# Register values of the tensor engine in rows of eight words, and an even share of aggregation behind every group, in a graph network kernel

## The chip, the core and the metric

The kernel runs on one core of a Trainium2 chip. The metric is the device time of one execution in microseconds, as the median of several runs. TensorE (PE) multiplies matrices, VectorE (DVE) does element-wise work and reductions, ScalarE (ACT) copies, scales and evaluates functions, GpSimd (POOL) sets constants up here, and SyncE (SP) starts most transfers. Each engine works through its own instructions in their order; semaphores tie the engines together. An instruction whose address is known only at run time takes it from a register, and a TENSOR_LOAD fills registers with values from on-chip memory.

## The reference: what is computed

3125 nodes with 128 features each, 53125 edges (src, dst, type), sorted by dst. Two blocks follow each other:

```
agg  = segment_sum((x[src] + rel_emb[type]) @ W_msg.T + b_msg, dst) / max(deg, 1)
x    = layernorm(x + x @ W_self.T + b_self + agg)
h    = swish(segment_mean(x[src], dst) @ W1_l.T + b1 + x @ W1_r.T)
out  = layernorm(x + segment_mean(h[src], dst) @ W2_l.T + b2 + h @ W2_r.T)
```

So one graph is used three times: three times a sum over each node's incoming edges, and behind each a small dense step.

## The kernel before

**Edges become a matrix of counts.** `A` (the profile calls it counts) holds in f16 how many edges lead from each source node to each destination node, 25 blocks of 128 sources by 3125 destinations. It is made from 416 tiles of 128 edges. Four tiles are a group, so there are 104 groups. For each group DVE writes one-hot rows (`one_hots`, L1165 to L1181) into one of two, from group 12 on one of three, buffers; it may refill a buffer when PE has signalled `released` for the group that used it. PE turns the rows into counts with some 20 small matmuls (`count`, L878 to L932: blocks L894, types L901, shared columns L910 and L930) in a window of PSUM, and ACT copies that window into `A` in two halves (L837), with `copied` signalled to PE.

**Run-time places.** Where a tile's 12 columns stand within the group's window of 38 is data. DVE computes it (L1128) into `place_i`, three int32 per group, for the tiles 1 to 3 (tile 0 always stands at 0). PE loads the values for two groups (`LOADED = 2`), six words or 24 bytes, ahead of every even group (L1040), 52 loads in all. ACT loads the first column of eight groups' windows at once (L828), eight words or 32 bytes. The built program puts `place_i` at an address that is a multiple of 32 bytes, so PE's loads start alternately on a multiple of 16 and on 8 bytes beside one.

**Work behind the groups.** As edges are sorted by destination, the first columns of `A` are complete long before the last group. `spread()` plans which blocks of the first aggregation (`aggregate`, L945: table block times counts, two matmuls of 256 columns per block, since the table holds each value as a high and a low part) stand behind which group. Five chunks of 512 nodes are cut into eleven parts of 256 columns, 25 blocks each. A part may start only from the group `READY[part] + 1` on. The number of blocks behind a group is `4 - group % 2`: four behind an even group, three behind an odd one, none behind the four groups of `OWN`, fewer where dense steps (`dense`, L1011 and L1021, `count_degrees`, L977) are planned behind the same group. When all 25 blocks of a part are placed, the next part waits for its `READY`. What has not been placed by group 103 is done right after the loop. The functions `lead`, `scale`, `root`, `normalise` of ACT and `degrees`, `add_up`, `measure`, `combine`, `invert`, `low` of DVE follow the groups given by that same plan.

**The rest.** After group 103 the other chunks and the two later layers run, 50 matmuls of 512 columns per chunk, with the dense steps between them. Four weights are loaded by SP into the memory of the one-hot rows when the last group has been copied (L705). Biases are loaded at the start (L699). A check that the plan holds for these edges runs on DVE (`check_edges`) while PE aggregates layer 1.

Of the kernel before, what the change touches and what calls it, by code (L numbers as in the profile page):

```python
# [15 lines left out]
P = 128  # L16
N = 3125
D = 128
# [63 lines left out]
def spread():  # L82
# [5 lines left out]
    for group in range(GROUPS):  # L88
        room = 0 if group in OWN else 4 - group % 2
# [92 lines left out]
def gnn_program(nc, x, src_t, dst_t, type_t, first_dst, rel_emb, w_msg, w_self, w1_l, w1_r,  # L182
                w2_l, w2_r, b_self, b_msg, b1, b2, x1_dram, h_dram, out):
    with ExitStack() as ctx:
# [5 lines left out]

        A = sb("counts", [P, BLOCKS, WIDTH], F16)
# [12 lines left out]
        base_i = sb("base", [P, GROUPS], I32)  # L204

        place_i = sb("place", [P, GROUPS, GROUP - 1], I32)
        weights_first = sb("weights_first", [P, 2, D])
        bias_rows = sb("bias_rows", [P, 3, D])
# [10 lines left out]
        std = sb("std", [P, SUB])  # L219
        offset = sb("offset", [P, SUB])  # L220
        eps_col = sb("eps_col", [P, 1])
        peaks = sb("peaks", [P, PEAKS])
        limits = sb("limits", [P, PEAKS])
        over = sb("over", [P, PEAKS])
        any_over = sb("any_over", [P, 1])
        ones_col = sb("ones_col", [P, 1])
        flag = sb("flag", [P, 1], I32)
# [23 lines left out]
        assert 4 * D + 2 * CHUNK + TILES + GROUPS <= (SLOTS - 1) * HOT_C * GROUP // 2  # L251

        ident = new_first[:, 0:P]
        bias_msg = scaled_flat[:, 0:D]

        def by_tile(buffer):
            return buffer.rearrange("p (g t) -> p g t", t=GROUP)
# [422 lines left out]
        def _(sp):  # L680
# [16 lines left out]
            for to, b in ((bias_rows[:, 0, :], b_self), (bias_msg, b_msg),  # L697
                          (bias_rows[:, 1, :], b1), (bias_rows[:, 2, :], b2)):
                sp.dma_start(to, b.rearrange("o d -> (o d)").partition_broadcast(P)  # L699
                             ).then_inc(weights_in, 16)  # L700
# [18 lines left out]
        def _(pool):  # L719
# [11 lines left out]
            nc.gpsimd.memset(peaks[:], 0.0)  # L731
            for at, most in ((slice(0, 1), (TILE_W - 1) / 2), (slice(1, 2), -1.0),
                             (slice(2, 3), 0.0), (slice(3, 5), float(TILE_W)),
                             (slice(5, 7), 0.0), (slice(7, 8), MOST_VALUE),
                             (slice(8, 9), MOST_EDGES / 2 - 1),
                             (slice(9, 10), (TYPE_W - 1) / 2),
                             (slice(10, PEAKS), MOST_VALUE / SCALE)):
                last = nc.gpsimd.memset(limits[:, at], most)
            last.then_inc(constants, 1)
# [139 lines left out]
        def _(pe):  # L879
# [116 lines left out]
            def dense(q, tiles):  # L996
                layer, size = layer_of(q), min(P, nodes_of(q))
                if 0 in tiles:
                    pe.wait_ge(sum_ready, q + 1)
                    pe.wait_ge(own_ready, max(q + 1, POSTED))  # L1000
                    if before(q) >= 0:
                        pe.wait_ge(messages_scaled, before(q) + 1)
                        if q >= POSTED:
                            pe.wait_ge(y_ready, before(q) + 1)
                    if q == CHUNKS:
                        pe.wait_ge(late_weights_in, 64)
                    if q >= POSTED:
                        pe.wait_ge(preset_done, q + 1 - POSTED)
# [29 lines left out]
            for group in range(GROUPS):  # L1038
# [5 lines left out]
                mine = group % LOADED * (GROUP - 1)  # L1044
                count(group, places[mine:mine + GROUP - 1])
# [44 lines left out]
        def _(dve):  # L1090
# [18 lines left out]
            def of_groups(count=GROUP):  # L1109
# [18 lines left out]
            nc.vector.tensor_tensor(place_i[:], by_tile(start_i)[:, :, 1:GROUP],  # L1128
                                    of_groups(GROUP - 1), ALU.subtract
# [65 lines left out]
            def constant(step):  # L1195
# [5 lines left out]
                elif step == 1:  # L1201
                    dve.wait_ge(weights_in, 16 * 6)
                    nc.vector.tensor_tensor(weights_first[:, 1, :], weights_first[:, 1, :],
                                            ident, ALU.add).then_inc(weights_ready, 1)
                elif step == 2:
                    nc.vector.tensor_tensor(bias_rows[:, 0, :], bias_rows[:, 0, :], bias_msg,
                                            ALU.add).then_inc(weights_ready, 1)
# [17 lines left out]
            def preset(q):  # L1225

                layer, size = layer_of(q), min(P, nodes_of(q))
                bias = bias_rows[0:size, layer, :]
# [17 lines left out]
            def store_own(q):  # L1246
# [6 lines left out]
                    bias_rows[:, 0, :].unsqueeze(1).to_broadcast([P, SUB, D]), ALU.add  # L1253
# [76 lines left out]
            def check_edges():  # L1330
# [14 lines left out]
                                               -(TILE_W - 1) / 2, place_i[:, 0:early],  # L1345
# [4 lines left out]
                                               place_i[:, early:GROUPS, 0:GROUP - 2],  # L1350
# [4 lines left out]
                                               place_i[0:REST, early:GROUPS, GROUP - 2],  # L1355
# [6 lines left out]
                for t in range(GROUP):  # L1362
# [23 lines left out]
                nc.vector.tensor_copy(within[:, :, 0], place_i[:, :, 0]).then_inc(check_step, 1)  # L1386
                nc.vector.tensor_tensor(within[:, :, 1:GROUP - 1], place_i[:, :, 1:GROUP - 1],
                                        place_i[:, :, 0:GROUP - 2], ALU.subtract
                                        ).then_inc(check_step, 1)
                nc.vector.tensor_tensor(steps[:, 0:early], steps[:, 0:early],  # L1390
                                        place_i[:, 0:early, GROUP - 2], ALU.subtract
# [9 lines left out]
                for h in range(EARLY_PARTS):  # L1401
# [13 lines left out]
                                        place_i[:, GROUPS - 1, GROUP - 2:GROUP - 1], ALU.subtract  # L1415
# [36 lines left out]
            for q in range(EARLY - 1, ALL_CHUNKS):  # L1452
                if EARLY <= q < CHUNKS:
                    degrees(q)
                if q == CHUNKS:
                    dve.wait_ge(agg_done, CHUNKS)
                    check_edges()
# [7 lines left out]
                if q == 2 * CHUNKS:  # L1465
                    dve.wait_ge(check_step, CHECKS + 1 + CHUNKS)
                    nc.vector.tensor_tensor(over[:], peaks[:], limits[:], ALU.is_gt
                                            ).then_inc(over_step, 1)
                    dve.wait_ge(over_step, 1)
                    nc.vector.tensor_reduce(any_over[:], over[:], AX.X, ALU.max  # L1470
# [61 lines left out]
```

## Time and profile before

| | us |
|---|---|
| median of 3 runs | 376.63 (376.56 to 378.17) |
| the profiled execution, its own time | 376.94 |
| its span, first to last instruction | 375.2 |
| PE busy | 340.1 (91%) |
| DVE busy | 239.5 (64%) |
| ACT busy | 175.2 (47%) |
| granted TensorE clock, mean | 0.992 of full speed |

The profiled execution is 1.74 us longer than its span and 0.31 us longer than the median. The shares over the span hide two very different stages: groups are counted from about 12 us to 189 us, where three engines are busy at once, and from there PE works nearly alone.

### The profile page before, as it was taken

What the parts mean: (1) busy time and instruction counts of PE and PEld (TensorE: products, weight loads), DVE (VectorE), ACT (ScalarE), POOL (GpSimd) and SP (SyncE); (2) the same over time, 40 slices, a digit from 0 to 9 for tenths busy, and PEclk for the clock granted to TensorE, in tenths of its full rate; (3) what the DMA queues carried; (4) which work ended last, traced back from release to release, by engine and by line L of the source; (5) the groups of instructions that cost most, each with busy time, mean ns of one, the idle gap of its engine ahead of it and who ended that gap; (6) DMA issues with size and microseconds to landing.
All of it is one profiled execution on the core that took longest, in us unless ns stands there. A gap on an engine that the chain in (4) does not pass through costs nothing.

```text
span 375.2 us, 9264 instructions
## 1 busy us (share of the span) xinstructions
PE 340.1 (91%) x3385; PEld 249.6 (67%) x3385; DVE 239.5 (64%) x666; ACT 175.2 (47%) x385; POOL 5.1 (1%) x26
## 2 busy tenths in 40 slices
PE   0579999998999999999899999999999999999980
PEld 0578898887888888888886445554565454555460
DVE  6999988988898998998635763303317013431445
ACT  1577666668767768668623204311334130221130
POOL 5000000000000000000000000000000000000000
PEclk9999999999999999999999999999999999999996
DMA  4700000000000000000010000000000000000102
GB/s 130 177 3 3 2 2 3 4 2 0 4 2 2 3 2 2 3 3 3 1 31 0 3 0 2 0 2 0 0 2 2 0 1 30 28 3 28 29 2 64
DMA packets 8523, 5.38 MB, mean 14 GB/s; under 512 B 370, under 2 KB 8476, under 8 KB 8476
## 3 DMA queue, kind: packets, MB, share of 16 engines
q1 hardware_dynamic: 8188, 4.32, 4.2%
q8 instruction: 31, 0.51, 0.6%
q10 hardware_dynamic: 288, 0.43, 0.5%
q14 instruction: 16, 0.13, 0.1%
HBM read 3.14 MB, written 1.60 MB: 13 GB/s over the span
## 4 chain that ended last, share of the span: by engine, by line
PE 80%; DVE 13%; issue 4%; ACT 1%; DMA 1%; DVEq 0%; ACTq 0%
PE ps L945 50%; PE ps L894 17%; PE ps L1011 5%; DVE hot L1181 3%; PE ps L1021 3%; PE ps L964 2%; DVE hot L1170 2%; DMA counts<-dst_t 1%; DVE table L1181 1%; PE ps L901 1%; PE ps L991 1%; PE ps L910 1%; DVE table L1191 1%; DVE stats L1276 1%; ACT scaled L793 1%
## 5 line engine op out<-in xcount | busy, mean ns | idle before, releaser
L945 PE MATMUL ps<-counts,table 128*128 128x256 f16 (+2 forms) x1350 | 215.7, 309 | 0.8 <-ACT sum_first L770 0.8
L945 PEld LDWEIGHTS ps<-counts,table 128*128 128x128 f16 x1350 | 114.3, 97 | 75.0 <-issue 1.1
L837 ACT CAST counts<-ps 128x494 f32 x208 | 107.6, 573 | 55.0 <-PE ps L894 54.6
L894 PE MATMUL ps<-hot 128*128 128x156 f16 (+1 forms) x584 | 70.4, 244 | 21.0 <-DVE hot L1181 15.2
L894 PEld LDWEIGHTS ps<-hot 128*128 128x128 f16 x584 | 53.4, 103 | 27.7 <-DVE hot L1181 16.5
L1181 DVE TENSOR_TENSOR hot<-iota,edges 128x1200 f16<-128x1200 f16 x73 | 56.6, 776 | 0.0
L1170 DVE TENSOR_TENSOR hot<-iota,edge_rows 128x768 f16<-128x768 f16 x73 | 40.3, 552 | 6.9 <-PE ps L930 6.6
L901 PE MATMUL ps<-hot 128*128 128x19 f16 x292 | 43.4, 181 | 0.0
L1269 DVE TENSOR_TENSOR new_first<-ps,scaled 128x512 f32<-128x512 f32 (+1 forms) x9 | 5.4, 599 | 54.0 <-ACT scaled L793 54.0
L1269 DVE TENSOR_TENSOR hot<-ps,scaled 128x512 f32<-128x512 f32 (+1 forms) x8 | 5.1, 638 | 41.9 <-ACT scaled L793 41.9
L894 PE MATMUL ps<-table 128*128 128x156 f16 (+1 forms) x248 | 28.8, 237 | 1.4 <-DVE hot L1181 0.5
L901 PEld LDWEIGHTS ps<-hot 128*128 128x128 f16 x292 | 29.2, 100 | 0.5
L770 ACT ACTIVATE sum_first<-ps 128x512 f32<-128x512 f32 (+1 forms) x13 | 7.0, 539 | 45.3 <-PE ps L945 45.3
L770 ACT ACTIVATE hot<-ps 128x512 f32<-128x512 f32 (+1 forms) x8 | 4.4, 548 | 48.1 <-PE ps L945 48.1
L793 ACT ACTIVATE scaled<-ps,rdeg 128x128 f32<-128x128 f32 (+1 forms) x75 | 21.6, 372 | 11.1 <-PE ps L1011 8.6
L894 PEld LDWEIGHTS ps<-table 128*128 128x128 f16 x248 | 21.8, 99 | 4.9 <-DVE hot L1181 2.2
L1181 DVE TENSOR_TENSOR table<-iota,edges 128x1200 f16<-128x1200 f16 x31 | 24.0, 775 | 0.0
L910 PE MATMUL ps<-next_hot,hot 128*128 128x13 f16 (+1 forms) x144 | 21.7, 185 | 0.0
L1170 DVE TENSOR_TENSOR table<-iota,edge_rows 128x768 f16<-128x768 f16 x31 | 17.1, 552 | 2.4 <-PE ps L930 2.1
L901 PE MATMUL ps<-table 128*128 128x19 f16 x124 | 17.8, 176 | 0.0
L910 PEld LDWEIGHTS ps<-next_hot,hot 128*128 128x128 f16 x144 | 14.4, 100 | 0.5
L1181 DVE TENSOR_TENSOR hot<-iota_type,edges 128x76 f16<-128x76 f16 x73 | 13.9, 190 | 0.0
(136 smaller groups left out, 320.1 us busy)
## 6 DMA issues: line engine op xcount, KB each, us to landing
table<-x SPq DMA_DIRECT2D x2, 768.0 KB, 5.2
out<-new_first SPq DMA_DIRECT2D x3, 256.0 KB
out<-hot SPq DMA_DIRECT2D x3, 256.0 KB, 2.3
counts<-first_dst ACTq DMA_DIRECT2D x1, 208.0 KB, 3.7
counts<-dst_t SPq DMA_DIRECT2D x1, 208.0 KB, 4.7
counts<-type_t ACTq DMA_DIRECT2D x1, 208.0 KB, 5.1
counts<-src_t SPq DMA_DIRECT2D x1, 208.0 KB, 5.2
bias_rows<-b SPq DMA_DIRECT2D x2, 64.0 KB, 4.4
```

What stands on the lines that cost most here:

```text
L770: nc.scalar.activation(sum_T(q)[:, 0:nodes], ps[:, sums_bank(q), 0:nodes], ACT.Copy, scale=1.0 / SCALE).then_inc(sum_ready, 1)
L793: last = nc.scalar.activation(scaled[0:part, t], ps[0:part, messages_bank(q), t * D:(t + 1) * D], ACT.Copy, scale=rdeg[0:part, tile:tile + 1])
L837: nc.scalar.copy(A[:, HALVES[half], bass.ds(bases[group % 8], GROUP_W)], window(group, half)).then_inc(copied[half], 1)
L894: return nc.tensor.matmul(window(group, half)[:, :, at[t]], row(tiles[t], LOW_AT, P), blocks_of(tiles[t], half), start=group == half == t ...
L901: return nc.tensor.matmul(relations(group)[:, column], row(tiles[t], TYPE_AT, P), row(tiles[t], WIN_AT, TYPE_W), start=group == t == 0, st ...
L910: nc.tensor.matmul(window(then, half)[:, :, 0:1], row(tiles[-1], LOW_AT, P), next_hot[:, group // NEXT % 2, HALVES[half], group % NEXT].un ...
L945: last = nc.tensor.matmul(ps[:, sums_bank(q), first:first + width], table[:, b, part, :], A[:, b, at:at + width], start=b == part == 0, st ...
L1011: sent = nc.tensor.matmul(ps[0:size, messages_bank(q), t * D:(t + 1) * D], sum_T(q)[:, at], weight(layer, 0), start=True, stop=True)
L1021: last = nc.tensor.matmul(to, own_T[:, at], weight(layer, 1), start=False, stop=False, skip_group_check=True)
L1170: nc.vector.tensor_tensor(rows[:, :, TYPE_AT + REL_ROW:M_AT, :].rearrange("p h (k c) t -> p h k c t", c=PIECE), iota[:, 0:PIECE, :].unsque ...
L1181: last = nc.vector.tensor_tensor(rows[:, :, at:at + width, :], numbers, edge[:, kind, group * GROUP:(group + 1) * GROUP].rearrange("p (h t ...
L1269: nc.vector.tensor_tensor(rows(new(q), q), from_own, rows(scaled, q), ALU.add).then_inc(y_ready, 1)
```

## The change

- `place_i` gets four int32 per group instead of three: the value of tile 0 is kept too (it is not used as an address). A row of two groups is eight words, 32 bytes, and PE's load takes all eight. `place_i` and `base_i` are moved in front of the other buffers; the built program puts `place_i` on a multiple of 32 bytes again, so every load starts on a multiple of 32 bytes.
- `spread()` has room for four blocks behind every group. 20 instead of 16 blocks of the eleventh part are placed inside the loop.
- To make room for it in memory, `b2` is no longer loaded at the start but after the four late weights, into the same memory as they; the wait of PE for these transfers and one of DVE take it in. `limits`, which POOL set at the start with nine memsets, lies in the memory of `next_block` and is set by DVE behind the seventh aggregation. Small buffers are put together. The check takes the extra word in: it multiplies the value of tile 0 by 128 and adds it to the next.

```diff
-        room = 0 if group in OWN else 4 - group % 2
+        room = 0 if group in OWN else 4
...
+        base_i = sb("base", [P, GROUPS], I32)
+
+        place_i = sb("place", [P, GROUPS, GROUP], I32)
         A = sb("counts", [P, BLOCKS, WIDTH], F16)
...
-        base_i = sb("base", [P, GROUPS], I32)
-
-        place_i = sb("place", [P, GROUPS, GROUP - 1], I32)
...
-        bias_rows = sb("bias_rows", [P, 3, D])
+        bias_first = sb("bias_rows", [P, 2, D])
...
+        bias_last = later[:, 4 * D + 2 * CHUNK + TILES + GROUPS:][:, 0:D]
...
+        limits = next_block[:].bitcast(F32)[:, 0:PEAKS]
...
             for k, w in enumerate((w1_l, w1_r, w2_l, w2_r)):
                 sp.dma_start(weights_later[:, k, :], w).then_inc(late_weights_in, 16)
+            sp.dma_start(bias_last, b2.rearrange("o d -> (o d)").partition_broadcast(P)
+                         ).then_inc(late_weights_in, 16)
...
-            nc.gpsimd.memset(peaks[:], 0.0)
-            for at, most in ((slice(0, 1), (TILE_W - 1) / 2), (slice(1, 2), -1.0),
...
-                last = nc.gpsimd.memset(limits[:, at], most)
-            last.then_inc(constants, 1)
+            nc.gpsimd.memset(peaks[:], 0.0).then_inc(constants, 1)
...
                     if q == CHUNKS:
-                        pe.wait_ge(late_weights_in, 64)
+                        pe.wait_ge(late_weights_in, 80)
...
-                mine = group % LOADED * (GROUP - 1)
-                count(group, places[mine:mine + GROUP - 1])
+                mine = group % LOADED * GROUP
+                count(group, places[mine + 1:mine + GROUP])
...
-            nc.vector.tensor_tensor(place_i[:], by_tile(start_i)[:, :, 1:GROUP],
-                                    of_groups(GROUP - 1), ALU.subtract
+            nc.vector.tensor_tensor(place_i[:], by_tile(start_i), of_groups(), ALU.subtract
                                     ).then_inc(place_ready, 1)
...
-                    dve.wait_ge(weights_in, 16 * 6)
+                    dve.wait_ge(weights_in, 16 * 5)
...
+                if q == 2 * CHUNKS:
+                    dve.wait_ge(late_weights_in, 80)
...
                 if q == CHUNKS:
                     dve.wait_ge(agg_done, CHUNKS)
+                    for at, most in ((slice(0, 1), (TILE_W - 1) / 2), (slice(1, 2), -1.0),
...
+                        nc.vector.memset(limits[:, at], most)
```

Two places on PE. The first is the end of group 15 and the start of group 16, before the change; table and hot are the buffers of one-hot rows, and x6 stands for six instructions alike.

```order
360 L894 ISA
361 L894 MATMUL ps<-table 128x12x12
362 L910 MATMUL ps<-next_hot,table 128x12 [waits copied1]
363 L930 MATMUL ps<-next_node,table 128x1
364 L945 MATMUL ps<-counts,table 128x256 x6
365 L1040 TENSOR_LOAD place
366 L894 MATMUL ps<-hot 128x13x12 [waits v_hot]
```

The same place after it:

```order
360 L890 ISA
361 L890 MATMUL ps<-table 128x12x12
362 L906 MATMUL ps<-next_hot,table 128x12 [waits copied1]
363 L926 MATMUL ps<-next_node,table 128x1
364 L941 MATMUL ps<-counts,table 128x256 x8
365 L1036 TENSOR_LOAD place
366 L890 MATMUL ps<-hot 128x13x12 [waits v_hot]
```

The load stands where it stood, between the aggregation of the odd group and the counting of the even one; two more matmuls of 256 columns stand ahead of it. The second place on PE is the end of the loop, before the change:

```order
2376 L894 ISA
2377 L894 MATMUL ps<-hot 128x12x12
2378 L945 MATMUL ps<-counts,table 128x256 x24
2379 L1032 MATMUL ps<-iota 128x512 [waits constants,copied1,copied0]
2380 L945 MATMUL ps<-counts,table 128x256 x50
```

And after it:

```order
2369 L890 ISA
2370 L890 MATMUL ps<-hot 128x12x12
2371 L941 MATMUL ps<-counts,table 128x256 x18
2372 L1028 MATMUL ps<-iota 128x512 [waits constants,copied1,copied0]
2373 L941 MATMUL ps<-counts,table 128x256 x50
```

Of the 24 matmuls six stood behind group 103 and 18 were what the loop had left; now eight stand behind group 103 and ten are left. So eight matmuls have moved into the loop. No instruction of PE is added or taken away.

## Rows read from the trace of the kernel before

**Rows 1.** Stretch, length, busy PE, PEld, DVE, ACT, POOL, clock, DMA share, GB/s.

```profile
34.00:186.00 152.00, 144.56 (x1970) 129.85 (x1968) 138.13 (x363) 108.96 (x229) 0.00 (x0) 1.00 0.01 2
...
206.00:375.20 169.20, 158.10 (x986) 87.43 (x984) 63.02 (x195) 41.77 (x105) 0.00 (x0) 0.98 0.04 11
```

**Rows 2.** Waits from 34 to 186 us: us in total, times, longest.

```profile
PEld ps L894 <- issue: 8.5, 17, 1.0
DVE hot L1170 <- PE ps L930: 6.3, 19, 0.7
PE ps L894 <- issue: 3.5, 5, 0.8
DVE next_hot L1165 <- PE ps L930: 2.9, 10, 0.5
PEld ps L894 <- DVE hot L1181: 2.6, 6, 0.7
DVE table L1170 <- PE ps L930: 2.1, 7, 0.5
PEld ps L894 <- DVE table L1181: 1.0, 1, 1.0
```

**Rows 3.** The chain of work, behind groups 19 to 22, 33 and 34: start, us, what.

```profile
48.09 0.68 PE ps L945 x6
49.51 0.90 PE ps L945 x8
51.16 0.68 PE ps L945 x6
52.97 0.90 PE ps L945 x8
...
70.90 0.68 PE ps L945 x6
71.58 0.65 issue
73.27 0.90 PE ps L945 x8
```

**Rows 4.** PE's loads: all, then one by one; ns min/median/max, first and last start.

```profile
L1040 PEldq TENSOR_LOAD <-place x52: 813/1240/1487, 8.3 to 184.6; - x52
...
L1040 PEldq TENSOR_LOAD <-place x1: 1474/1474/1474, 70.7 to 70.7; - x1
...
L1040 PEldq TENSOR_LOAD <-place x1: 814/814/814, 161.4 to 161.4; - x1
```

**Rows 5.** ACT's loads of eight words from 20 us on.

```profile
L828 ACTq TENSOR_LOAD <-base x12: 544/546/549, 28.3 to 175.6; - x12
```

**Rows 6.** Timeline: group 46's last one-hot row, and PE's first matmul of it.

```profile
89.30 0.19 DVE L1181 TENSOR_TENSOR hot<-iota_type,edges 128x76 f16<-128x76 f16 x1
...
92.47 0.23 PE L894 MATMUL ps<-hot 128*128 128x156 f16 x1 [0.73 <-DVE table L1181]
```

**Rows 7.** DVE's groups by line: busy, mean ns.

```profile
L1123 DVE TENSOR_TENSOR counts<-counts,base 128x416 int32<-128x416 int32 x1 | 0.6, 586 | 0.0
L1128 DVE TENSOR_TENSOR place<-counts,base 128x312 int32<-128x312 int32 x1 | 0.5, 473 | 0.0
```

**Rows 8.** The end of the loop, in order of time.

```profile
187.75 1.16 ACT L793 ACTIVATE scaled<-ps,rdeg 128x128 f32<-128x128 f32 x4
188.54 2.79 PE L945 MATMUL ps<-counts,table 128*128 128x256 f16 x24
188.76 1.07 ACT L837 CAST counts<-ps 128x494 f32 x2
```

**Rows 9.** A late weight's transfer: KB each, us to landing.

```profile
hot<-w_r SPq DMA_DIRECT2D x2, 64.0 KB, 2.0
```

**Rows 10.** Timeline of DVE in a chunk's first dense step.

```profile
101.89 0.69 DVE L1269 TENSOR_TENSOR new_first<-table,scaled 128x512 f32<-128x512 f32 x1
...
103.77 0.86 DVE L1276 BATCH_NORM_STATS2 stats<-new_first 128x6 f32<-128x128 f32 x4
```

More of the change, by code:

```diff
@@ L218, in gnn_program @@
         moments = sb("moments", [P, SUB, 2])
-        std = sb("std", [P, SUB])
-        offset = sb("offset", [P, SUB])
-        eps_col = sb("eps_col", [P, 1])
+        small = sb("small", [P, 16])
+        std, offset = small[:, 0:SUB], small[:, SUB:2 * SUB]
+        eps_col, any_over, ones_col = (small[:, k:k + 1] for k in range(8, 11))
+        flag = small[:, 11:12].bitcast(I32)
         peaks = sb("peaks", [P, PEAKS])
[L223 to L227, printed above, removed]
         stage_x = table1[:].rearrange("p b s d -> p (b s d)").bitcast(F32).rearrange(
@@ L250, in gnn_program @@
         steps = later[:, 4 * D + 2 * CHUNK + TILES:4 * D + 2 * CHUNK + TILES + GROUPS]
-        assert 4 * D + 2 * CHUNK + TILES + GROUPS <= (SLOTS - 1) * HOT_C * GROUP // 2
+        bias_last = later[:, 4 * D + 2 * CHUNK + TILES + GROUPS:][:, 0:D]
+        assert 5 * D + 2 * CHUNK + TILES + GROUPS <= (SLOTS - 1) * HOT_C * GROUP // 2
         ident = new_first[:, 0:P]
         bias_msg = scaled_flat[:, 0:D]
+        limits = next_block[:].bitcast(F32)[:, 0:PEAKS]
+        over = stats[:].rearrange("p t s -> p (t s)")[:, 0:PEAKS]
         def by_tile(buffer):
@@ L696, in _ @@
                 sp.dma_start(weights_first[:, k, :], w).then_inc(weights_in, 16)
-            for to, b in ((bias_rows[:, 0, :], b_self), (bias_msg, b_msg),
-                          (bias_rows[:, 1, :], b1), (bias_rows[:, 2, :], b2)):
+            for to, b in ((bias_first[:, 0, :], b_self), (bias_msg, b_msg),
+                          (bias_first[:, 1, :], b1)):
                 sp.dma_start(to, b.rearrange("o d -> (o d)").partition_broadcast(P)
@@ L1227, in preset @@
                 layer, size = layer_of(q), min(P, nodes_of(q))
-                bias = bias_rows[0:size, layer, :]
+                bias = bias_last[0:size] if layer == 2 else bias_first[0:size, layer, :]
+                if q == 2 * CHUNKS:
+                    dve.wait_ge(late_weights_in, 80)
                 if tiles_of(q) > 1:
@@ L1384, in check_edges @@
                 dve.wait_ge(check_step, 9)
[L1386 to L1388 removed]
+                nc.vector.scalar_tensor_tensor(within[:, :, 0], place_i[:, :, 0], float(P),
+                                               place_i[:, :, 1], ALU.mult, ALU.add
+                                               ).then_inc(check_step, 1)
+                nc.vector.tensor_tensor(within[:, :, 1:GROUP - 1], place_i[:, :, 2:GROUP],
+                                        place_i[:, :, 1:GROUP - 1], ALU.subtract
                                         ).then_inc(check_step, 1)
                 nc.vector.tensor_tensor(steps[:, 0:early], steps[:, 0:early],
[L1391 removed]
+                                        place_i[:, 0:early, GROUP - 1], ALU.subtract
                                         ).then_inc(check_step, 1)
@@ L1466, in _ @@
                     dve.wait_ge(check_step, CHECKS + 1 + CHUNKS)
-                    nc.vector.tensor_tensor(over[:], peaks[:], limits[:], ALU.is_gt
+                    nc.vector.tensor_tensor(over, peaks[:], limits, ALU.is_gt
                                             ).then_inc(over_step, 1)
                     dve.wait_ge(over_step, 1)
-                    nc.vector.tensor_reduce(any_over[:], over[:], AX.X, ALU.max
+                    nc.vector.tensor_reduce(any_over[:], over, AX.X, ALU.max
                                             ).then_inc(any_ready, 1)
```

22 lines of the change are left out of this document (11 added, 11 removed).

## The prediction

> **What bounds the kernel now.** I read the busy time by stretch first. From 34 to 186 us, where the groups are counted, PE is busy for 144.56 of 152 us, DVE for 138.13 and ACT for 108.96 [rows 1]: PE leads, but DVE follows by only 6.4 us. After 206 us DVE is busy for 63 of 169 us, so there only PE's own work counts. PE's granted clock is 1.00 in the first of these stretches, the upper of its two levels (2.4 GHz), and 0.98 in the last.
>
> Next, the waits of the counting stage [rows 2]. The weight loads ahead of a group's first matmul stood idle 24 times (17 + 6 + 1), 12.1 us in all (8.5 + 2.6 + 1.0). 17 times the profile names "issue", that is, nothing it can see; 7 times it names DVE. I don't believe the seven: the last one-hot row of group 46 was written at 89.49 us, and PE began that group at 92.47, 3 us later, after 0.73 us of idle time [rows 6]. And DVE itself waits for PE (L930 signals `released`) 36 times, 11.3 us: it runs ahead and is stopped by the full buffers. So in this stage DVE is not what PE waits for.
>
> What is, the chain of waits and the loads show together. The stage has 24 waits, and every second even group is one. PE's 52 loads of six words come in two kinds, about 0.81 us and about 1.47 us [rows 4] (814 ns at 161.4 us, 1474 at 70.7 us, the median of all between the two). They alternate, since a row of 24 bytes starts alternately on a multiple of 16 bytes and 8 bytes beside one. In the chain [rows 3] the aggregation behind group 19 starts at 48.09 and that behind 20 at 49.51: 1.42 us with a short load between them. From 51.16 (group 21) to 52.97 (group 22) it is 1.81 us, with a long load between. The work in both steps is alike: six matmuls of 256 columns, then one group's counting. So a long load costs 0.39 us there, and a short one nothing, since the queued matmuls of the odd group cover it. At group 34 the cover is thinner: 70.90 to 73.27 is 2.37 us, 0.95 more than with a short load, with 0.65 of it as "issue". The load there starts at 70.7 us and ends at 72.17, and the first matmul follows at 72.23.
>
> **The loads, worked out.** Dear ones: the 5 waits of PE named "issue" (3.5 us in all [rows 2], 0.7 each), and two that were put down to DVE, as that of group 46: 7 × 0.95 = 6.7 us. The other 17: 17 × 0.39 = 6.6 us. Together 13.3 us, the most that PE can get back here if no load sticks out.
>
> How long does a load of eight words take? PE has none, but ACT has: eight words from a multiple of 32 bytes take 0.544 to 0.549 us, twelve times over [rows 5]. The changed kernel's loads are the same in size and alignment, only on another sequencer. From above the nearest row is PE's own long load scaled by words, 1.474 / 6 × 8 = 1.97 us; from below 0.544. I take 0.55, the row that is like it in everything but the engine, and since PE's short loads too are nearer to it than to 1.97. A load of 0.55 us in place of one of 1.47 ends 0.92 us sooner. That is more than the 0.39 us that the usual long load sticks out, and about the 0.95 of the dear ones. The schedule adds cover: two more matmuls of 256 columns stand ahead of most loads, and eight take 0.90 us [rows 3], so 0.22 us. So no load should stick out.
>
> One rule speaks against it. The Trainium skill, in "Runtime: NRT & Kernel Launch", section "Instruction fetch mechanics", says that a TENSOR_LOAD takes some 200 ns for each register, also in bulk. ACT's rows say 68 ns a word for eight, PE's say 136 (short) and 246 (long), so the rule fits only the long ones. By it every load would take an estimated 1.6 us; what that gives stands with the rivals.
>
> **The schedule.** Four blocks behind every group move eight matmuls of 256 columns, 0.9 us, from behind the loop into it. PE's instructions stay the same, so while PE is the bound this is worth nothing. It pays up to 0.9 us where PE would otherwise wait for DVE. The price is on the other side: a part is finished sooner and then waits for `READY`, so more groups have no block behind them, and in those PE catches up with DVE. At the loop's end less work covers the last copies: ACT ends them at 189.83 (188.76 + 1.07), 1.3 us after PE began the last 24 matmuls at 188.54 [rows 8]; 18 take 2.0 us, so they still cover them. I take 0, and keep -0.9 and +1.
>
> **What DVE leaves of it.** DVE is idle for 152 - 138.1 = 13.9 us of the stage [rows 1]. If PE gives back 13.3, DVE has 0.6 us left over the whole stage. The two loads are then even, and with three buffers neither can run far ahead; wherever DVE has a chunk's dense step to do between two groups (0.69 and 0.86 us for its first two parts [rows 10]), PE will now and then wait. There are five such chunks. I take 0.3 us for each, 1.5 us; the bounds are 0 and 5 × (0.69 + 0.86) = 7.8 us, when each pair is fully exposed.
>
> **The small edits.** L1128 computes 416 words instead of 312, ahead of the first group; a like operation takes 586 ns with 416 and this one 473 with 312 [rows 7]: +0.1 us, exposed. The bias loaded late lands about 2.0 us behind its issue [rows 9], near 194 us; PE's wait stands before the first dense step of layer 1, past 206 us, and DVE's before layer 2: 0. Were the cover gone it would cost the 2.0 us of a landing. Nine memsets on DVE come where it is idle for 106 of 169 us [rows 1]: 0. Fewer memsets on POOL and one transfer less at the start: nobody waits there, 0.
>
> **The sum.** -13.3 (loads) + 1.5 (DVE) + 0.1 (L1128) = -11.7 us, on a profiled execution of 376.94 us: 365.2. That execution lies 0.3 us over the median, 376.63, so the forecast for the median is 364.9, and I say 365.
>
> **The rivals.**
>
> A: *the engines that become the bound take more of it.* For it: DVE's margin of 0.6 us; ACT is busy for 109 of a stage that shrinks to 140 us, and a chunk's four scalings hold its copies up for 1.16 us [rows 8], which PE can meet before the next group but one. Against it: DVE is over 2 us ahead of PE now, and is stopped by the buffers. If each of five chunks costs 1.16 us for ACT beside DVE's 0.3, 5.8 us are lost: about 371.
>
> B: *the parity is not one of addresses* but of the registers that the loads alternate between, and eight words keep it: every second load stays at 1.47 us. Only the added cover helps, 0.22 us for 24 loads, 5.3 us: about 371 too. For it: the trace shows alternation alone. Against it: ACT's twelve loads of eight words don't alternate, and the addresses do, in just this step.
>
> C: *words set the price; slower.* Every load takes 1.97 us. The 24 long ones stick out by 0.55 us on average now (13.3 / 24); each of 46 would by 0.55 + 0.50 - 0.22 = 0.83 us, 38.2 us in place of 13.3: 376.6 + 24.9, about 401. It decides from the length at which 46 × (L - 1.47 + 0.55 - 0.22) is 13.3 us, L = 1.43 us. Against it: rows 5, a third of that. By the skill's 200 ns a word, 1.6 us each, the same sum gives an estimated 384.
>
> D: *no change that can be seen*: loads are quick, but the waits named "issue" have another cause that stays. Against it: at group 34 the first matmul follows the end of the load by 0.06 us, and so it should be at each.
>
> **How the numbers follow.** Forecast 0.75; A 0.14; B 0.04; C 0.04; D 0.03. The likeliest case's own range goes from 361 (13.3, 0.9 of the schedule, and some of the short loads' remainders) to 368.5. Toward A and B it reaches up to 370; what is left out is C, D, the far end of A, and a little below, under 2 in 10. Faster by over 0.5% (below 374.7; 0.5% is about what a measurement can tell) 0.93, within it 0.03, slower 0.04.
>
> **What would show it.** PE's loads: 52 of about 0.55 us, all alike (B: still two kinds; C: about 2). The waits "PEld L894 <- issue" of the stage gone, and in the chain about 1.65 us from one aggregation of eight matmuls to the next, over a load or not. DVE's waits for L930 down from 11.3 to a few us, and new, true waits of PE for DVE or ACT in places, 1 to 3 us. The last group counted at about 177 us in place of 188.5. From there to the end the same 186 us as before, less up to 0.9. The prediction is wrong if loads are uniform and short and the time still stays above 370: then DVE or ACT holds more than I read; and if it falls below 361, PE's counting was slowed by the loads in more than their gaps.

## The result and the profile after

The changed kernel takes 367.08 us (median of four runs, 365.98 to 367.65) beside 377.40 us for the kernel before on the same chip. The ratio is 0.9722 with a 95% interval of 0.9681 to 0.9763: faster by 2.8%. The forecast was 365, the range 361 to 370. The profiled execution took 366.55 us, with a span of 364.7 us and a mean granted clock of 0.986; PE is busy for 333.9 us of it, DVE for 237.7 and ACT for 173.8.

The counting stage after, in the columns of [rows 1] (stretch, length, busy PE, PEld, DVE, ACT, POOL, clock, DMA share, GB/s):

```profile
34.00:175.00 141.00, 138.06 (x1952) 128.98 (x1952) 134.79 (x360) 106.16 (x225) 0.00 (x0) 1.00 0.01 2
```

It is idle for 2.94 us on PE, where [rows 1] left 7.44. The loads, as in [rows 4]:

```profile
L1036 PEldq TENSOR_LOAD <-place x52: 587/590/780, 8.2 to 175.0; - x52
...
L824 ACTq TENSOR_LOAD <-base x13: 536/546/744, 5.7 to 166.6; - x13
...
L1124 DVE TENSOR_TENSOR place<-counts,base x1: 585/585/585, 7.4 to 7.4; 128x416 int32<-128x416 int32 x1
```

The 52 loads are of one kind, 0.59 us (the first, at 8.2 us, took 0.78). The two kinds of before are gone. The waits of that stage (us in total, times, longest), as in [rows 2]:

```profile
PEld ps L906 <- ACT counts L833: 2.3, 8, 0.6
DVE next_hot L1160 <- PE ps L926: 1.9, 7, 0.5
PEld ps L890 <- DVE hot L1176: 1.5, 3, 0.5
DVE hot L1165 <- PE ps L926: 1.3, 5, 0.3
PE ps L890 <- DVE hot L1176: 1.3, 3, 0.4
...
DVE table L1165 <- PE ps L926: 0.6, 2, 0.3
...
PE ps L906 <- ACT counts L833: 0.5, 1, 0.5
PE ps L890 <- DVE table L1176: 0.4, 1, 0.4
```

The "issue" waits are gone, DVE's waits for the released buffer are 3.8 us in place of 11.3, and a new wait leads among PE's: the last shared columns (L906) for ACT's copies. (A wait of the weight load and one of the matmul behind it are two rows for one place, so they are not added up.) In the chain (start, us, what) the steps are now even, 1.65 us with a load or without one, where [rows 3] has 1.42 and 1.81:

```profile
40.41 0.90 PE ps L941 x8
...
42.06 0.90 PE ps L941 x8
...
43.71 0.90 PE ps L941 x8
...
45.34 0.90 PE ps L941 x8
```

To see where time went I cut each traced execution at two instructions that all kernels share: PE's first matmul of group 14, and its first of group 103, the last group. "Opening" is what lies before the first, "rest" what follows the second. The column "lost" adds up what PE lost around the counting of groups 14 to 102: by how much the gap ahead of a group's first matmul was over its usual -0.16 us (matmuls overlap), and by how much the counting was over 0.91 us. It doesn't count waits inside the aggregation. All columns are worked out from the times of the matmuls, in us.

| kernel | opening | groups 14 to 103 | rest | span | lost |
|---|---|---|---|---|---|
| before | 38.8 | 149.1 | 187.3 | 375.2 | 15.7 |
| changed | 37.9 | 140.1 | 186.7 | 364.7 | 7.3 |
| e1: changed rows, old plan | 37.8 | 136.5 | 187.3 | 361.6 | 3.0 |
| e2: old rows, changed plan | 38.5 | 152.1 | 186.6 | 377.3 | 18.4 |
| e5: a single load | 39.1 | 140.2 | 186.7 | 365.9 | 7.0 |
| e7: loads earlier | 37.9 | 139.9 | 186.7 | 364.5 | 7.1 |
| e8: e7 with the old plan | 38.0 | 136.6 | 187.3 | 361.8 | 3.1 |
| e9: smooth plan | 39.3 | 134.1 | 188.0 | 361.3 | 1.8 |
| e10: less work for ACT | 37.9 | 138.8 | 186.7 | 363.4 | 6.1 |
| e11: e10 with the old plan | 39.5 | 135.5 | 187.3 | 362.3 | 2.2 |
| e12: less work for DVE | 39.0 | 140.1 | 186.6 | 365.7 | 7.3 |

The middle is where the change acts: 149.1 to 140.1. Three of the plan's four extra blocks stand ahead of group 103, and make the rest 0.6 us shorter. The opening varies between kernels that are alike in it; what the traces show of that stands at the end.

### The profile page after: what moved, and what is told of

Read it like the earlier page. It is cut to its first block, busy times and chain, and to the rows that moved or that the text cites. A ratio compares the mean times of both kernels' runs of the same rounds, so it can differ in the third digit from the quotient of the medians.

```text
span 364.7 us, 9265 instructions
## 1 busy us (share of the span) xinstructions
PE 333.9 (92%) x3385; PEld 249.3 (68%) x3385; DVE 237.7 (65%) x675; ACT 173.8 (48%) x385; POOL 4.8 (1%) x17
## 4 chain that ended last, share of the span: by engine, by line
PE 83%; DVE 10%; ACT 3%; issue 1%; DMA 1%; ACTq 0%; DVEq 0%
PE ps L941 54%; PE ps L890 16%; PE ps L1007 5%; PE ps L1017 3%; DVE hot L1176 2%; PE ps L960 2%; DVE hot L1165 1%; ACT counts L833 1%; DMA counts<-dst_t 1%; PE ps L897 1%; PE ps L906 1%; DVE table L1186 1%; PE ps L987 1%; ACT scaled L789 1%; DVE new_first L1301 1%
## 5 line engine op out<-in xcount | busy, mean ns | idle before, releaser
L890 PE MATMUL ps<-hot 128*128 128x156 f16 (+1 forms) x584 | 67.5, 241 | 16.7 <-DVE hot L1176 16.0
L890 PEld LDWEIGHTS ps<-hot 128*128 128x128 f16 x584 | 52.8, 103 | 18.7 <-DVE hot L1176 16.7
L897 PE MATMUL ps<-hot 128*128 128x19 f16 x292 | 42.1, 180 | 0.0
L897 PEld LDWEIGHTS ps<-hot 128*128 128x128 f16 x292 | 28.9, 99 | 0.7
L890 PE MATMUL ps<-table 128*128 128x156 f16 (+1 forms) x248 | 27.6, 235 | 0.9 <-DVE hot L1176 0.9
L766 ACT ACTIVATE sum_first<-ps 128x512 f32<-128x512 f32 (+1 forms) x13 | 7.0, 542 | 44.8 <-PE ps L941 44.8
L766 ACT ACTIVATE hot<-ps 128x512 f32<-128x512 f32 (+1 forms) x8 | 4.4, 548 | 47.7 <-PE ps L941 47.7
L789 ACT ACTIVATE scaled<-ps,rdeg 128x128 f32<-128x128 f32 (+1 forms) x75 | 21.7, 373 | 11.1 <-PE ps L1007 8.6
L906 PE MATMUL ps<-next_hot,hot 128*128 128x13 f16 (+1 forms) x144 | 21.6, 184 | 1.0 <-ACT counts L833 0.5
L906 PEld LDWEIGHTS ps<-next_hot,hot 128*128 128x128 f16 x144 | 14.2, 99 | 2.5 <-ACT counts L833 2.1
L799 ACT ACTIVATE small<-moments,small 128x4 f32<-128x4 f32 (+1 forms) x14 | 4.2, 303 | 20.5 <-DVE moments L1282 20.5
```

Source lines behind the costliest of these rows:

```text
L766: nc.scalar.activation(sum_T(q)[:, 0:nodes], ps[:, sums_bank(q), 0:nodes], ACT.Copy, scale=1.0 / SCALE).then_inc(sum_ready, 1)
L789: last = nc.scalar.activation(scaled[0:part, t], ps[0:part, messages_bank(q), t * D:(t + 1) * D], ACT.Copy, scale=rdeg[0:part, tile:tile + 1])
L890: return nc.tensor.matmul(window(group, half)[:, :, at[t]], row(tiles[t], LOW_AT, P), blocks_of(tiles[t], half), start=group == half == t ...
L897: return nc.tensor.matmul(relations(group)[:, column], row(tiles[t], TYPE_AT, P), row(tiles[t], WIN_AT, TYPE_W), start=group == t == 0, st ...
L906: nc.tensor.matmul(window(then, half)[:, :, 0:1], row(tiles[-1], LOW_AT, P), next_hot[:, group // NEXT % 2, HALVES[half], group % NEXT].un ...
```

## The experiments

### One half of the change at a time

**e1_rows_only** is the changed kernel with the old plan:

```diff
-        room = 0 if group in OWN else 4
+        room = 0 if group in OWN else 4 - group % 2
```

> The changed kernel with the old plan (4 and 3 blocks in turn). Theory: the loads carry the gain; 52 loads of 0.59 us, time 365.5 to 368, within 1 us of the changed kernel, or even up to 1 us faster, since fewer odd groups stand without a block. Rival (the plan is worth its share): 369 or more.

Measured: 364.17 us (363.39 to 364.92), ratio 0.9646 (0.9619 to 0.9673). It is better than the whole change, and 1.3 us below the range that I had given. Its last group begins at 174.30 us, that of the changed kernel at 177.98, and that of before at 187.87 (38.81 + 149.06). PE's first matmul of that group, first in the changed kernel:

```profile
177.98 0.23 PE L890 MATMUL ps<-hot 128*128 128x156 f16 x1
```

and in e1:

```profile
174.30 0.23 PE L890 MATMUL ps<-hot 128*128 128x156 f16 x1
```

The rows of eight words, with the small edits that come with them, are thus worth 13.6 us up to the last group (12.6 of them between groups 14 and 103, 1.0 in the opening), and the plan takes 3.7 back. The stage in e1, and of its waits PE's for the copies, for ACT's copy of a chunk's sums inside the aggregation, and for nothing seen:

```profile
34.00:175.00 141.00, 139.86 (x1998) 131.07 (x1996) 134.30 (x361) 109.63 (x233) 0.00 (x0) 1.00 0.01 3
```

```profile
PEld ps L906 <- ACT counts L833: 1.0, 4, 0.3
...
PE ps L941 <- ACT sum_first L766: 0.8, 2, 0.4
...
PEld ps L890 <- issue: 0.2, 1, 0.2
```

PE is idle for 1.1 us there, against 2.9 in the changed kernel. What the plan takes back can be split only roughly. Six matmuls of 256 columns more stand between groups 14 and 103, 0.65 us by PE's 0.109 us for each, and that is given back behind the last group. PE's losses around the counting grow by 4.3 us (7.3 against 3.0). The 0.8 us of waits inside the aggregation fall away. That makes 4.2 us, where 3.6 were measured between the two groups.

**e2_plan_only** is the kernel before with room for four blocks, the same line the other way round.

> The kernel before with four blocks behind every group, loads of six words kept. Theory: PE is the bound, so moving its work is worth nothing: 375.5 to 377.5. Rival B of the prediction (cover is what pays): 0.22 us for each of 24 long loads, about 371 to 372.

Measured: 380.63 us (379.15 to 382.07) beside 377.81 for the kernel before in the same rounds, ratio 1.0088 (1.0061 to 1.0115): slower by 2.8 us, or 0.9%, which neither theory had. The plan costs time without the rows too, about 3 us. Group by group its loss sits elsewhere than before: at group 78, for one, PE loses 1.67 us where it lost 0.48. One part of the traced loss is not the plan's: between 120 and 124 us the granted clock fell.

```profile
116.00:120.00 4.00, 2.80 (x39) 2.23 (x36) 3.82 (x10) 4.00 (x10) 0.00 (x0) 1.00 0.02 4
120.00:124.00 4.00, 3.96 (x36) 3.66 (x37) 2.64 (x9) 1.31 (x4) 0.00 (x0) 0.57 0.01 2
```

From the start of group 60 to that of group 64 it took 9.1 us, where the kernel before takes 6.8. Up to 2.3 us of this one trace can thus be the clock's; the plan's own losses at groups 61 and 62 are in them too. The medians carry the verdict, not this trace.

### What sets the length of a load

**e3_shift8** and **e4_shift4** are the kernel before with the buffer of the values moved by 8 and by 4 bytes:

```diff
-        place_i = sb("place", [P, GROUPS, GROUP - 1], I32)
+        place_flat = sb("place", [P, GROUPS * (GROUP - 1) + 2], I32)
+        place_i = place_flat[:, 2:].rearrange("p (g t) -> p g t", t=GROUP - 1)
```

(`+ 1` and `1:` in e4.)

> The kernel before with the places' buffer begun 8 bytes later. Theory (address decides): still 26 long and 26 short loads, but the long ones are now those of the groups 0, 4, 8, ..., and the short ones those of 2, 6, ...; time as before, 376 to 379. Rival (the order of loads or registers decides): the same loads as before are long.

> The kernel before with the places' buffer begun 4 bytes later, so that no load starts on a multiple of 8 bytes. Theory (whole aligned pieces are fetched at once, the rest word by word): all 52 loads are long, 1.47 us or more; time 384 to 392. Rival: two kinds still, time as before.

Measured, a single execution each: 376.36 us and 386.49 us. In e3 the two kinds have changed places. The load ahead of group 20, before a short one, and that ahead of group 22, before a long one:

```profile
L1041 PEldq TENSOR_LOAD <-place x1: 1475/1475/1475, 46.7 to 46.7; - x1
...
L1041 PEldq TENSOR_LOAD <-place x1: 817/817/817, 50.3 to 50.3; - x1
```

In e4 all are long:

```profile
L1041 PEldq TENSOR_LOAD <-place x52: 1462/1467/1651, 8.3 to 193.9; - x52
```

So for loads of six words it is the start address that decides, not the registers (rival B): from a multiple of 16 bytes they take 0.82 us, from 8 or 4 bytes beside one 1.47. Eight words from a multiple of 32 take 0.59, fewer than six do, so the time doesn't grow with the number of words (rival C) either. But the start address isn't all. Rows of 24 bytes begin, at every second short load, on a multiple of 32 bytes too, and all short loads from 14 us on take 0.81 to 0.83 us. Eight words from such an address are quicker than six. No run here loads eight words from another address, or explains how the words are fetched.

### Do the loads that are left still cost anything?

The gap ahead of a group's first matmul, usually -0.16 us, is another size in four places: in the changed kernel that ahead of groups 28, 44, 78 and 96 is 0.43 us, and a load fills it. **e5_one_load** loads once, ahead of group 0, and uses those values throughout, so the counts stand in wrong columns:

```diff
-                if group % LOADED == 0:
+                if group == 0:
```

> The changed kernel with a single load on PE, at group 0, whose values serve all groups (so the counts stand in wrong columns; the work is the same). Theory: 51 loads of 0.59 us cost PE only where they follow a group without blocks behind it, groups 28, 44, 78 and 96, and part of the 1.0 us lost at each is ACT's lateness: 1.5 to 3.5 us less than the changed kernel, 363.5 to 365.5. Rival (the loads still cost everywhere): 360 or less. Rival (ACT's copies alone hold those places): no change.

Measured: 367.65 us (365.90 to 368.11), ratio 0.9725 (0.9680 to 0.9770), against 0.9722 for the changed kernel: no gain. **e7_early** keeps the loads and moves those that follow an odd group with at most one block and no other work behind it, nine of them from group 14 on, ahead of that group's counting:

```diff
+                elif group + 1 < GROUPS and bare(group):
+                    coming = load(group + 1)
```

> The changed kernel with the loads that follow an odd group with at most one block behind it moved ahead of that odd group's counting. Theory: the loads of 0.59 us stand out only there, so 1 to 3 us less than the changed kernel. Rival: these places wait for ACT's copies anyway, no change.

Measured: 366.93 us (366.04 to 367.54), ratio 0.9720 (0.9679 to 0.9760): no gain either. With the old plan, **e8_early_old_plan**:

> The same early loads with the old plan (4 and 3 blocks in turn), which had 364.2 us with its loads in place. Theory: that plan leaves few such places, group 28 above all, so 0 to 1 us less, 363.2 to 364.5. Rival: no early load helps, since the load now stands between the even group's blocks and the odd group's counting: 364.2 or more.

Measured: 364.27 us (363.32 to 365.15), ratio 0.9652 (0.9610 to 0.9695), e1's time. That lies in the theory's range and in the rival's, so it decides nothing by itself.

The timelines of group 44 say why. Columns: start, us, engine, line and operation, shapes, idle time before it and what ended that. In the changed kernel PE is held twice, first by the load (0.43 us; DVE, which is named, had written the group's last row at 83.12), and again between the last two shared columns:

```profile
82.93 0.19 DVE L1176 TENSOR_TENSOR hot<-iota_type,edges 128x76 f16<-128x76 f16 x1
...
84.08 0.16 PE L926 MATMUL ps<-next_node,hot 128*128 128x1 f16 x1
84.68 0.23 PE L890 MATMUL ps<-hot 128*128 128x156 f16 x1 [0.43 <-DVE table L1176]
...
85.48 0.25 PE L890 MATMUL ps<-hot 128*128 128x144 f16 x1
85.83 0.19 PE L906 MATMUL ps<-next_hot,hot 128*128 128x12 f16 x1
85.88 0.16 PE L926 MATMUL ps<-next_node,hot 128*128 128x1 f16 x1
```

In e7 the group begins 0.58 us sooner and ends at the same time (ACT's row among PE's):

```profile
84.07 0.16 PE L926 MATMUL ps<-next_node,hot 128*128 128x1 f16 x1
...
84.10 0.23 PE L890 MATMUL ps<-hot 128*128 128x156 f16 x1
...
84.72 1.05 ACT L833 CAST counts<-ps 128x494 f32 x2
...
85.37 0.19 PE L906 MATMUL ps<-next_hot,hot 128*128 128x13 f16 x1 [0.48 <-ACT counts L833]
...
85.87 0.16 PE L926 MATMUL ps<-next_node,hot 128*128 128x1 f16 x1
```

Its last matmul stands at 85.87, 85.88 with the late load. (The rows between are PE's other small matmuls and its weight loads.) What PE waits for is ACT: the columns that group 44 shares with group 45 may be written only when group 43's window has been copied, and that copy runs from 84.72 to 85.77. In e5 the same wait is the largest of PE's in the stage, 16 times at the weight load and 10 times at the matmul:

```profile
PEld ps L906 <- ACT counts L833: 6.1, 16, 0.6
...
PE ps L906 <- ACT counts L833: 3.0, 10, 0.5
```

### Which engine holds those places?

ACT's timeline over the same groups in the changed kernel:

```profile
82.94 1.05 ACT L833 CAST counts<-ps 128x494 f32 x2 [0.25 <-PE ps L890]
83.87 0.61 ACT L766 ACTIVATE sum_first<-ps 128x512 f32<-128x512 f32 x1
84.34 0.50 ACT L811 ACTIVATE new_first<-new_first,small 128x128 f32<-128x128 f32 x1
84.73 1.05 ACT L833 CAST counts<-ps 128x494 f32 x2
85.63 0.53 ACT L811 ACTIVATE new_first<-new_first,small 128x128 f32<-128x128 f32 x1
```

Between two pairs of copies stands the copy of a finished chunk's sums (L766, 0.61 us) and a quarter of the last chunk's normalisation (L811, 0.50). **e10_act_less** leaves out three of the four activations of such a normalisation, 12 in all (ACT's instructions fall from 385 to 373), and **e11_act_less_old_plan** does the same with the old plan:

```diff
+                    if t + 1 < SUB:
+                        continue
```

> The changed kernel, ACT's normalisation of the first four chunks left out for three of four tiles (their rows stay as they are, so the output is another): twelve activations of some 0.3 us less on ACT. Theory: ACT's lateness holds PE at the bare groups 28, 44, 61, 78 and 96, so this gives back 1.5 to 3.5 us: 363.5 to 365.5. Rival (ACT isn't what PE waits for there): no change, 366.5 to 367.5.

> The same left out with the old plan and the new rows (364.2 us as it stands). Theory: few bare groups, so PE waits little for ACT there: 0 to 1 us less, 363.2 to 364.2. Rival (ACT's work costs PE everywhere): as much as in the changed kernel.

Measured: e10 365.04 us (364.86 to 366.62), ratio 0.9680 (0.9641 to 0.9720); e11 362.64 us (361.96 to 364.06), ratio 0.9600 (0.9564 to 0.9636). That is 2.0 and 1.5 us by the medians, with intervals that overlap those of the changed kernel and of e1, and 1.3 and 1.0 between groups 14 and 103 of the traces. The gain in e10 stands where the theory puts it (group 44 loses 0.74 us in place of 1.05, group 61 0.65 in place of 1.02, group 78 0.70 in place of 1.02, and group 95 0.19 in place of 0.56; groups 28 and 96, which I had named too, stay at 0.74 and 1.01), and PE's wait for the copies, 2.3 us in the changed kernel, is 1.4:

```profile
PEld ps L908 <- ACT counts L835: 1.4, 6, 0.3
```

But I had expected 0 to 1 us with the old plan, and it gains nearly as much there. So these activations are a small load under either plan, and don't alone explain what the plan costs.

For DVE, **e6_dve_less** left out its one-hots of the types from the fourth group on:

```diff
+                    if kind == FROM_BASE and hot_before(group) >= 0:
+                        continue
```

> The changed kernel without the one-hot rows of the edge types from the fourth group on (the old rows stay in their buffers; the type part of the counts is wrong), some 0.11 us less of DVE's work for each of 101 groups, 11 us in all. Theory: after group 14 DVE is not the bound of the changed kernel, and up to there, where it is, it saves 0.11 us a group: 1 to 2.5 us less. Rival (DVE is the new bound of the whole stage): 5 us less or more.

Measured: 22562.72 us. The kernel's own test of the plan for these edges failed with the altered counts, and it took its general path: the number says nothing of the question. **e12_dve_less2** is the same edit with the thresholds of that test raised:

```diff
-                        nc.vector.memset(limits[:, at], most)
+                        nc.vector.memset(limits[:, at], 1e30)
```

> The changed kernel without the one-hot rows of the edge types from the fourth group on, its fallback's thresholds lifted so that it isn't taken: 11 us less of DVE's work in the counting stage. Theory: DVE bounds only the first 14 groups, where 0.11 us a group are saved: 1 to 2 us less, 365 to 366. Rival (DVE is the bound that the 1.5 us of the prediction stood for, or more): 3 us less or more.

Measured: 367.39 us (367.20 to 368.61), ratio 0.9740 (0.9702 to 0.9777): no gain, not even the 1 to 2 us that I had expected of the first 14 groups. DVE is busy for 8.4 us less of the stage, PE for 0.01 us more, so nothing:

```profile
34.00:175.00 141.00, 138.07 (x1946) 128.93 (x1947) 126.39 (x270) 106.23 (x227) 0.00 (x0) 1.00 0.01 2
```

```profile
DVE hot L1165 <- PE ps L926: 5.8, 18, 0.4
DVE next_hot L1160 <- PE ps L926: 4.0, 11, 0.6
PEld ps L906 <- ACT counts L833: 2.7, 10, 0.5
DVE table L1165 <- PE ps L926: 2.3, 8, 0.4
```

What DVE saved, it waits: 12.1 us for PE (5.8 + 4.0 + 2.3), where it waited 3.8. PE's wait for ACT stays.

### A plan with no empty groups

Where PE loses time in the changed kernel follows from the plan. From group 14 on it leaves nine groups with neither a block nor a dense step behind them: 27, 43, 52, 60, 69, 77, 86, 94 and 95. (Behind 94 stands a short other piece, the turning of a chunk's own rows at L960.) PE's loss in the group right behind each is 0.79, 1.05, 0.29, 1.02, 0.38, 1.02, 0.32, 0.56 and 1.02 us, together 6.5 of its 7.3. The old plan has three such groups (27, 61, and 95 with that same short piece), and in e1 PE loses 0.47 and 0.71 us behind the first two. A group with nothing behind it takes PE 0.75 us, and ACT 1.04 for its copies and DVE 1.27 for its one-hots.

Not all nine cost the same. Behind 52, 69 and 86 a part has just been completed in the middle of a chunk, and ACT does nothing there but its copies of the counts. At group 53, first matmul at 98.67 us:

```profile
97.16 1.05 ACT L833 CAST counts<-ps 128x494 f32 x2 [0.62 <-PE ps L890]
98.57 1.96 ACT L833 CAST counts<-ps 128x494 f32 x4 [0.37 <-PE ps L890]
```

There PE loses 0.3 to 0.4 us. Behind 27, 43, 60 and 77 a whole chunk is complete, ACT also copies that chunk's sums (L766), and PE loses 0.8 to 1.05. Behind 94 it loses 0.56, and behind 95, where ACT copies a chunk's own rows (L774) and normalises, 1.02. So the nine are costly mainly where ACT's work for a chunk falls on them.

**e9_smooth** places three blocks instead of four wherever three are enough to end the part by the time the next may start:

```diff
+        room = 0 if group in OWN else 4 - group % 2
+        if room and part + 1 < EARLY_PARTS:
+            rest = [g for g in range(group, READY[part + 1] + 1) if g not in OWN]
+            busy = sum(w[1] for w in waiting if w[0] <= READY[part + 1])
+            if BLOCKS - block <= 3 * len(rest) - busy:
+                room = 3
```

No group from 14 on is left without a block or other work. (Behind 99 and 101, the two that my expectation counts, stands a tile of a dense step, as behind 97 and 99 in the old plan.)

> The changed kernel with a plan that puts three blocks behind a group as soon as the part can still be finished that way before the next may start: 2 groups from 14 on without blocks or other work (99 and 101 near the end), against 9 in the changed kernel and 3 with the old plan. Theory (bare groups let PE catch up with ACT, and it then waits): as fast as the old plan with the new rows (364.2) or up to 1.5 us faster, 362.7 to 364.3. Rival (the number of bare groups doesn't matter): 366 to 368.

Measured: 362.86 us (361.36 to 363.16), ratio 0.9599 (0.9561 to 0.9636), the fastest complete kernel here: 4.2 us better than the changed kernel. Over e1 it is 1.3 us, and the two intervals overlap. Its stage, and of its waits that for the copies:

```profile
34.00:175.00 141.00, 140.61 (x2013) 132.17 (x2011) 135.26 (x364) 111.50 (x235) 0.00 (x0) 1.00 0.01 3
```

```profile
PEld ps L911 <- ACT counts L838: 0.5, 2, 0.3
```

PE is idle for 0.4 us of 141, and its waits for the copies are down from 2.3 us to 0.5. The price is 1.3 us more behind the last group (188.0 against 186.7), since fewer blocks are placed inside the loop, and 6.0 us less are spent in it. (Twelve matmuls fewer stand in it than in the changed kernel, 1.3 us of the 6.0.)

## Why the prediction was right, and where it was not

**The loads, -13.3 us: right.** e1, which has this part and the small edits alone, begins its last group 13.6 us sooner than before, 12.6 of it between groups 14 and 103; by the medians of its rounds it is 13.6 too (377.81 against 364.17). The loads take 0.59 us where 0.55 was taken from ACT's, and are uniform. Nearly no load sticks out: one wait named "issue" of 0.2 us is left in e1.

**The schedule, 0 with bounds of -0.9 and +1: the term that was mis-sized.** It costs 3.7 us before group 103 (140.11 + 37.87 against 136.49 + 37.81) and gives back 0.6 behind it, +3.0 in all; by medians 367.08 against 364.17, 2.9. The text named the price ("more groups have no block behind them, and in those PE catches up with DVE") and then cut it to the end of the loop. What it should have done is count those groups in both plans, nine against three, set the 0.75 us that PE takes there beside the 1.04 of ACT's copies and 1.27 of DVE, and look which of ACT's work for a chunk falls on them. The bounds came from PE's own work and the last copies, neither of which is this cost. e2 shows it with the old loads, where it is a loss of 2.8 us, and e9 takes it away and more.

**DVE, +1.5 us with bounds of 0 and 7.8: it measured 0.** e12 gives DVE 8.4 us and PE takes none. The engine that PE waits for in these places is ACT, through the copies. So the reasoning "PE will now and then wait" was right in kind, and 1 to 3 us of waits were forecast; the profile has eight of a weight load for ACT, 2.3 us. The four that it puts down to DVE (1.3 + 0.4 us at the matmul) are the load's gaps: at group 44 the rows had been there for 1.6 us (83.12) when PE began (84.68), and with DVE's work cut nothing is gained. The margin of 0.6 us that this term came from was also too small. From 34 us to the last group DVE's busy time before is still 138.13 us, in 153.8, so 15.7 less 13.3, or 2.4 us, would have been left by the prediction's own working. Measured, it is 143.9 - 135.5 = 8.4 us in the changed kernel, and 139.3 - 135.3 = 4.0 in e9, where the groups take the least time.

**L1128, +0.1 us: right in duration** (0.585 us in place of 0.473), though group 0 does not begin later than before for it, 12.28 against 12.44 us. The late bias and the memsets show nowhere.

**The sum.** -13.6 + 3.0 = -10.6 us; the spans differ by 10.5, 375.2 against 364.7. The forecast of -11.7 was near in part by luck: the plan's 3.0 us, which it had at 0, and the 1.5 us of DVE, which never came, stand on opposite sides. By the medians the forecast was 2.1 us too low, and 0.8 of that is the kernel before itself, whose median was 376.63 then and 377.40 beside the changed kernel.

**The rivals.** A put this loss on DVE and ACT at the chunks, with 1.16 us of ACT for each. The engine is right, and PE does lose most where ACT's work for a chunk meets a group with nothing behind it. But the four scalings that A named (L789) stand elsewhere, behind the second group after the last dense step of a chunk, and at groups 30 to 32, 47 to 49, 64 to 66 and 81 to 83 PE loses nothing. Of what does meet such groups, e10 shows 1.3 to 2.0 us for 12 activations. B falls with the uniform loads and with e3, and its time with e2. C falls with the 590 ns: by words it would have been 1.97 us. The 200 ns a register of the Trainium skill ("Runtime: NRT & Kernel Launch", section "Instruction fetch mechanics"), a page that speaks of register loads from HBM, gave an estimated 1.6 us a load; PE's eight words from on-chip memory took 74 ns each. The nearest to it is 245 ns a word in e4 (1467 / 6), where no load starts on a multiple of 16 bytes. D falls with the waits named "issue", which are gone with the long loads.

**What was to be seen:** uniform loads, no "issue" waits, 1.65 us steps, DVE's waits down to a few us (3.8) and the last group at about 177 us (177.98) all came. The rest is 186.7 us.

**What stays open.** That groups with nothing behind them carry the plan's price rests on e9 and on the places of the loss, and that most of it is ACT's work for a chunk on the places alone. How it divides there between ACT's copies, its copy of the sums and its other work is not: leaving out 12 activations gives much the same under both plans, and no run here takes the copies of the counts or of the sums away. And e5's 0.43 us gaps were replaced by waits of the same size, so the load's gap costs nothing now; with the copies out of the way it might.

## What to carry to other kernels

When an alternation in time fits an alternation in address, align the smallest thing that is loaded, even by loading words that aren't needed: six words cost 1.47 us or 0.82, and eight 0.59. Before you make work denser in front of a point where it has to wait for data, count the steps that are left without cover, and compare in those each engine's own time, with the occasional work that falls on them. A gap that a load fills need not be what it costs: move the load first (e7), and see whether the end of the group moves.

## What the runs showed of the hardware

On PE's queue the length of a load of six words depends on where it starts, and eight words from a multiple of 32 bytes are quicker than six from any address tried, as shown above; ACT's eight words took 0.546 us, 0.04 less than PE's.

The opening differs by up to 1.7 us between kernels that are alike in it. In the changed kernel TensorE's granted clock fell to its lower level for part of 20 to 24 us, after 4 us in which PE had been busy for 2.71:

```profile
16.00:20.00 4.00, 2.71 (x39) 2.38 (x36) 4.00 (x11) 4.00 (x9) 0.00 (x0) 1.00 0.00 0
20.00:24.00 4.00, 3.18 (x36) 2.97 (x37) 4.00 (x10) 2.92 (x7) 0.00 (x0) 0.57 0.02 6
```

In e11 it stayed there longer, and group 14 begins 1.6 us later than in the changed kernel:

```profile
20.00:24.00 4.00, 3.20 (x34) 2.99 (x35) 4.00 (x10) 2.90 (x7) 0.00 (x0) 0.51 0.02 6
24.00:28.00 4.00, 3.23 (x29) 3.15 (x28) 4.00 (x10) 2.24 (x4) 0.00 (x0) 0.50 0.00 0
```

The difference arises at one place: groups 0 to 7 begin within 0.05 us of each other in the two traces, and group 8 at 29.21 us in place of 27.62. Behind group 7 eight matmuls in f32 (L987 in the changed kernel) took 2.05 us in e11 and 1.14 in the changed kernel. In e5, e9 and e12, the other kernels with the new rows that open later than 38.5 us, they took 2.05 us as well. In e5 and e9 the rows show a clock of 1.00 there all the same, but their traces hold no record of the clock before 28.6 and 28.9 us, which is about where group 8 begins. So for these two the clock as the cause is not shown, though PE's pace is the same as in e11.

The same fall stands in e2 at 120 us, behind 4 us with 2.80 busy. The executions of one kernel spread by about as much (1.7 us for the changed kernel). So differences of 1 us between single traces were read from the part between groups 14 and 103 only.
